# The deformable loop on clamped ramps times differences of z, with one clamp pass out of PSUM, all products of a step in one block, and a pipelined offsets stage

## What is computed

```
# off: 9 offsets (taps) for each pixel, from a depthwise conv, batch norm, relu and a 1x1 conv
def dsc_axis(x, offset, weight, axis):        # axis 'x' moves along w, 'y' along h
    ix = wb + off   (or iy = hb + off)        # position to read on the pixel's own line
    s = grid_sample_zeros(x, ix, iy)          # linear between the two neighbours, zero outside
    return einsum('bchwk,ock->bohw', s, weight)
```

## Time and profile before

| | us |
|---|---|
| median of 3 runs | 5520.23 (5514.65 to 5533.72) |
| the profiled execution: first to last instruction | 5466.7 |
| TensorE busy | 4359.0 (80%) |
| VectorE, ScalarE, GpSimd busy | 2938.9, 2478.8, 2313.4 |
| granted TensorE clock, mean | 0.854 of 2.4 GHz |
| deformable, first to last product | 1992.2 to 4979.1 |
| offsets, first load to the last store landed | 1675 to 1938 |

### The profile page before, as it was taken

One profiled execution on the slowest core, in us unless ns is written; L12 is line 12 of the kernel. 1 busy time (PEld: TensorE's weight loads), 2 busy tenths in 40 slices (PEclk: granted clock), 3 DMA queues, 4 the chain that ended last, 5 costly groups with the idle time before them and its releaser, 6 DMA issues. The chain is left out here.

```text
span 5466.7 us, 153704 instructions
## 1 busy us (share of the span) xinstructions
PE 4359.0 (80%) x59170; PEld 2491.1 (46%) x59170; DVE 2938.9 (54%) x5592; ACT 2478.8 (45%) x2871; POOL 2313.4 (42%) x1844
## 2 busy tenths in 40 slices
PE   7765584379995549999999999999999899994188
PEld 6664453323332225555555555555555555552032
DVE  5206464423333437666766766676677667665411
ACT  5401143312223426656656666566566656663111
POOL 0002100100002347767767767677677667673000
PEclk9856696589997769989889989899799999897599
DMA  3456599987774640322023203203212231015877
GB/s 94 84 107 193 126 260 265 292 204 214 214 220 166 188 74 6 61 46 53 18 42 59 52 3 61 50 2 65 46 31 38 44 57 37 18 41 154 251 172 168
DMA packets 757030, 583.81 MB, mean 107 GB/s; under 512 B 36272, under 2 KB 695216, under 8 KB 746576
## 3 DMA queue, kind: packets, MB, share of 16 engines
q1 hardware_dynamic: 604424, 419.51, 33.3%
q10 hardware_dynamic: 141984, 121.83, 7.3%
q0 software_dynamic: 9984, 33.56, 1.9%
HBM read 371.84 MB, written 202.93 MB: 105 GB/s over the span
## 5 line engine op out<-in xcount | busy, mean ns | idle before, releaser
L1412 POOL TENSOR_SCALAR df_t<-df_t 128x1536 f32<-128x1536 f32 (+1 forms) x1536 | 2042.6, 1341 | 915.0 <-ACT df_t L1452 657.0
L1452 ACT ACTIVATE df_t<-df_a 128x1024 f32<-128x1024 f32 x1536 | 1574.6, 1025 | 1136.7 <-PE df_a L1604 1113.0
L1644 PE MATMUL df_o<-df_t,df_zs 128*32 128x128 f32 x36864 | 1432.8, 291 | 64.1 <-issue 57.8
L1488 DVE TENSOR_SCALAR df_t<-df_d 128x512 int32<-128x512 int32 x1536 | 1061.0, 691 | 672.5 <-PE df_d L1604 644.8
L1644 PEld LDWEIGHTS df_o<-df_t,df_zs 128*32 128x32 f32 x36864 | 985.8, 115 | 747.7 <-issue 581.0
L1627 PE MATMUL df_z<-net_Z,df_x 32*128 32x288 f32 x4096 | 876.2, 465 | 8.1 <-DVE df_zs L1500 4.6
L1604 PE MATMUL df_a<-df_ix,net_sel 17*128 17x512 bf16 x3072 | 632.1, 406 | 27.2 <-issue 26.3
L1604 PE MATMUL df_d<-df_ix,net_sel 17*128 17x512 bf16 x1536 | 613.6, 399 | 34.6 <-DVE df_t L1488 33.5
L1627 PEld LDWEIGHTS df_z<-net_Z,df_x 32*128 32x128 f32 x4096 | 419.8, 197 | 144.9 <-DVE df_zs L1500 84.7
L1500 DVE COPY df_zs<-df_z 128x576 f32<-128x576 f32 x512 | 382.6, 747 | 4.4 <-PE df_z L1627 4.4
L1458 ACT ACTIVATE df_zs<-df_z 128x576 f32<-128x576 f32 x512 | 331.0, 646 | 62.1 <-PE df_z L1627 60.0
(11 more groups left out here) (211 smaller groups left out, 4262.2 us busy)
## 6 DMA issues: line engine op xcount, KB each, us to landing
r_x<-x SPq DMA_DIRECT2D x64, 512.0 KB, 14.3
x<-r_x ACTq DMA_DIRECT2D x64, 512.0 KB, 11.2
gc_x<-x SPq DMA_DIRECT2D x240, 128.0 KB, 4.4
dc_x<-x SPq DMA_DIRECT2D x240, 128.0 KB, 3.2
dc_xt<-x_2t SPq DMA_DIRECT2D x240, 128.0 KB, 4.7
lc_x<-x SPq DMA_DIRECT2D x112, 256.0 KB, 5.2
fw_x<-in_x SPq DMA_DIRECT2D x32, 512.0 KB, 6.6
iv_x<-in_x SPq DMA_DIRECT2D x64, 256.0 KB, 4.8
```

The costliest lines, as they stand in the source:

```text
L1412: g.tensor_scalar(t, t, 1.0, 0.0, ALU.min, ALU.max).then_inc(hat_p, 1)
L1452: act.activation(t, ps_a[(m + i) % 2][:], ACT.Abs).then_inc(a_read, 1)
L1488: v.tensor_scalar(T[:, m % 2, 3 * i + 2].bitcast(I32), ps_d[:].bitcast(I32), 0x7fffffff, None, ALU.bitwise_and).then_inc(d_read, 1)
L1644: mm = pe.matmul(ps_o[32 * q:32 * q + 32, 0:P], Zs[:, m % 2, q, 32 * k:32 * k + 32], T[:, m % 2, 3 * i + x, P * q:P * q + P], start=(k == ...
```

## The change

**The algebra.** max(0, 1 - |d|) summed over grid points against z is the same as z at the first point times one ramp plus clamped ramps min(max(d, 0), 1) times the differences of neighbouring z. So the lines are made into differences `X[:, j+1] - X[:, j]` before `make_z`, the ramp needs a relu and a cap (or one clamp), and the absolute value, the line sums, `WS` and `S` go. The first point needs 4 more products a step: `apply_first` with `Z0` (9 rows x 32 columns for each line) and `E`, the offsets clamped to 0..1 in fp32, which `offsets` now stores as `edge`. Its four products have tile positions (32q, 32q). The grid row is in the constant, so the contraction has 16 rows instead of 17.

**The steps.** VectorE clamps 4 taps as two passes of 128x1024 and one tap as a pass of 128x512, straight from PSUM; ScalarE does the other 4 taps with a relu in two passes of 128x1024 and GpSimd caps them in two of 128x1024; ScalarE copies all of z out. `ps_a`, `ps_d` and `ps_z` have one buffer each. A quarter of the steps with a = 0 turn four lines at once (`turn`, `keep`), the others none. GpSimd prepares the lines of the next half (steps 10 to 19) instead of VectorE. All loops over images are unrolled.

**The queue.** Offsets and `E` come in quarters of a half, 24 steps ahead of use (runs of 2 KB and 4 KB). The lines of the next half are loaded at the start of a half, ahead of the trip of `uy`. `move_first` sends z of the first points through DRAM at step 21.

**offsets** is unrolled and pipelined over 4 PSUM banks: ScalarE writes the bf16 part from PSUM, the bias is a third matmul with 2 rows (`gl`, `gr`), VectorE clamps `HE`, and subtracts out of PSUM, two chunks deep; the next image is loaded when TensorE has read the one before.

TensorE in `deformable`, before: one step (df_o are the products, df_a and df_d the distances of a later step, df_z the z of the next; the rows between are register work).

The core of the diff, first `offsets` (ScalarE, TensorE, VectorE):

```diff
-                        for e in range(2):
-                            for m, co in enumerate((cox, coy)):
-                                h = HI[:, k, m, N // 2 * e:N // 2 * (e + 1)]
-                                a.activation(h, h, ACT.Relu, bias=co[:, 1:2], scale=co[:, 0:1]).then_inc(relu, 1)
-                        for c in range(NCH):
-                            n = b * NCH + c
-                            a.wait_ge(full, n + 1)
-                            a.wait_ge(low, n + 1)
-                            a.activation(t_o[:, c % 2], ps_f[c % 4][:], ACT.Identity, bias=wt["pb"][:, 0:1]).then_inc(taken, 1)
...
+                    a.activation(parts[:, k, 0, r], ps_f[n % NB][:], ACT.Copy).then_inc(high, 1)
+                    if b + 1 < B and c in (3, 6):
+                        rectify(b + 1, c // 6)
...
+                    for m in range(2):
+                        pe.matmul(ps_f[n % NB][:], wt["PW"][:, m, :], HI[:, b % 2, m, 512 * c:512 * c + 512],
+                                  start=(m == 0), stop=False)
+                    pe.matmul(ps_f[n % NB][:], wt["gl"][:], wt["gr"][:], start=False, stop=True).then_inc(full, 1)
...
+                        v.tensor_scalar(HE[:, k, r], ps_f[n % NB][:], 0.0, 1.0, ALU.max, ALU.min).then_inc(edged, 1)
+                        if n >= NB:
+                            v.wait_ge(low, n - NB + 1)
+                        v.tensor_tensor(t_r[:, n % NB], ps_f[n % NB][:], parts[:, k, 0, r], ALU.subtract).then_inc(rest, 1)
```

Then `deformable`, the readers of PSUM on ScalarE and VectorE:

```diff
-                    act.activation(t, ps_a[(m + i) % 2][:], ACT.Abs).then_inc(a_read, 1)
...
+                    act.activation(t, ps_a[:], ACT.Relu).then_inc(a_read, 1)
...
-                    v.tensor_scalar(T[:, m % 2, 3 * i + 2].bitcast(I32), ps_d[:].bitcast(I32), 0x7fffffff, None,
-                                    ALU.bitwise_and).then_inc(d_read, 1)
...
+                    t = T[:, n % 2, 4 * i + 2:4 * i + 4].rearrange("p k n -> p (k n)")
+                    v.tensor_scalar(t, ps_d[:], 0.0, 1.0, ALU.max, ALU.min).then_inc(d_read, 1)
```

And its TensorE:

```diff
+                    if 2 * n + i:
+                        pe.wait_ge(a_read, 2 * n + i)
+                    for x, tap in enumerate(SCALAR[i]):
+                        mm = spread(n, tap, ps_a[:, 512 * x:512 * x + 512])
+                    mm.then_inc(a_full, 1)
...
+                    for q in range(4):
+                        pe.matmul(ps_o[32 * q:32 * q + 32, 0:P], Z0[32 * q:32 * q + K9, hh % 2, C * j:C * j + C],
+                                  E[32 * q:32 * q + K9, P * j:P * j + P], start=False, stop=False, tile_position=(32 * q, 32 * q))
...
+                    if n + 1 < ST:
+                        fill_single(n + 1)
+                        fill_scalar(n + 1, 1)
+                        fill_vector(n + 1, 1)
+                        make_z(n + 1, 1)
+                    if n >= 0:
+                        if turn_due(n) or first_due(n):
+                            pe.wait_ge(s_read, n + 2)
+                        if turn_due(n):
+                            turn(n)
...
+                        apply(n, VECTOR[0] + SCALAR[0], True, False).then_inc(half, 1)
+                        apply_first(n)
+                        apply(n, (SINGLE,) + VECTOR[1] + SCALAR[1], False, True).then_inc(applied, 1)
+                    if n + 2 < ST:
+                        fill_scalar(n + 2, 0)
+                        fill_vector(n + 2, 0)
+                        make_z(n + 2, 0)
```

More of the change, by code:

```diff
@@ new lines, in deformable @@
+        ones, prep = s.sem("ones"), s.sem("prep")
+        a_full, a_read, clipped = s.sem("a_full"), s.sem("a_read"), s.sem("clipped")
+        d_full, d_read, s_full, s_read = s.sem("d_full"), s.sem("d_read"), s.sem("s_full"), s.sem("s_read")
+        z_full, z_read, half, applied, o_read = (s.sem(n) for n in ("z_full", "z_read", "half", "applied", "o_read"))
+        turned, kept, first, first_read = (s.sem(n) for n in ("turned", "kept", "first", "first_read"))
+        z0_out, z0_in = s.sem("z0_out"), [s.sem(f"z0_in{k}") for k in range(2)]
@@ L1337, in deformable, with turns, first_due @@
+        def turns(n):
+            return sum(turn_due(m) for m in range(n + 1))
+        def first_due(n):
+            return 0 <= n and place(n)[3] == 21 and place(n)[2] + 1 < NH
         with s.block() as block:
@@ L1594, in _, with keep @@
-                with v.Fori(0, B - 1) as b:
-                    image(b, True)
-                with v.Fori(B - 1, B) as b:
-                    image(b, False)
+                        v.tensor_tensor(U[:, j], ps_o[:, 0:P], U[:, j], ALU.add).then_inc(o_read, 1)
+                def keep(n):
+                    v.wait_ge(turned, turns(n))
+                    b, a, hh, j = place(n)
+                    g = (j // 4 - 1) % 8
+                    if g == 0 and b:
+                        v.wait_ge(uy_out, 64 * b)
+                    v.tensor_copy(YB[:].rearrange("h (o l) -> h o l", o=C)[:, :, 16 * g:16 * g + 16],
+                                  ps_s[:].rearrange("h (l o) -> h o l", o=C)).then_inc(kept, 1)
@@ L1599, in _ @@
+                for c in (6, 7):
+                    stats(B - 1, c)
             @block.tensor
             def _(pe):
[L1601 to L1613 removed]
@@ L1690, in _, with spread @@
-                with pe.Fori(B - 1, B) as b:
-                    image(b, False)
+                def spread(n, tap, out):
+                    b, a, hh, j = place(n)
+                    if j % QL == 0:
+                        pe.wait_ge(q_in[j // QL], 96 * (hh + 1))
+                    e, k = divmod(tap, SLOTS)
+                    g = 32 * (2 * (j // 16) + e)
+                    return pe.matmul(out, wt["sel"][g:g + K, k, :], ixv[g:g + K, :, P * (j % 16):P * (j % 16) + P], start=True, stop=True)
@@ new lines, in make_first, with turn @@
+                def make_first(hh):
+                    pe.wait_ge(prep, 11 * hh + 2)
+                    for q in range(4):
+                        r = slice(32 * q, 32 * q + 32)
+                        mm = pe.matmul(ps_s[r, 0:N9], X0[r, hh % 2, :], WZ[r, hh % 2, :], start=True, stop=True, tile_position=(32 * q, 32 * q))
+                    mm.then_inc(first, 1)
+                def turn(n):
+                    pe.wait_ge(o_read, n)
+                    for i in range(4):
+                        mm = pe.transpose(ps_s[:, P * i:P * i + P], XO[:, (n - 4 + i) % 8], wt["eye"][:])
+                    mm.then_inc(turned, 1)
@@ new lines, in apply, with apply_first @@
+                def apply(n, taps, start, stop):
+                    for i, k in enumerate(taps):
+                        for q in range(4):
+                            mm = pe.matmul(ps_o[32 * q:32 * q + 32, 0:P], Zs[:, n % 2, q, 32 * k:32 * k + 32],
+                                           T[:, n % 2, slot(k), P * q:P * q + P],
+                                           start=(start and i == 0), stop=(stop and i == len(taps) - 1))
+                    return mm
+                def apply_first(n):
+                    b, a, hh, j = place(n)
+                    if j == 0:
+                        pe.wait_ge(z0_in[hh % 2], 64 * (hh // 2 + 1))
+                    for q in range(4):
+                        pe.matmul(ps_o[32 * q:32 * q + 32, 0:P], Z0[32 * q:32 * q + K9, hh % 2, C * j:C * j + C],
+                                  E[32 * q:32 * q + K9, P * j:P * j + P], start=False, stop=False, tile_position=(32 * q, 32 * q))
```

724 lines of the change are left out of this document (306 added, 418 removed).

## The result

The changed kernel takes 5644.1 us (median of 4 runs, 5621.9 to 5655.6) against 5517.4 us for the kernel before in the same comparison (5509.4 to 5533.7). The ratio is 1.0226, with a 95% interval of 1.0190 to 1.0261: it is 2.3% slower. The forecast was 5362 us and "faster"; its range ended at 5585. The profiled execution has a span of 5642.0 us.

What follows compares the result with a forecast made beforehand. TensorE, busy 80% of the span, was taken as the bound. Steps +76, stops and low clock -202, offsets -18, start -12, weights -2 sum to -158: 5520.2 becomes 5362 us; own range 5290 to 5450, eight in ten 5220 to 5585.

Steps and rivals of the forecast that it cites:

- the undisturbed step: TensorE's deformable step without stops: 2.7 us to the products plus a 2.57 us block, 5.27 us; +76 us in eight images.
- The second fill for ScalarE: In a deformable step, TensorE's second distances for ScalarE start at 1.50 us, after waiting 0.3 us for its pass.
- VectorE's pair pass: VectorE's pass over 1024 columns of distances in a deformable step: taken as 1.2 us, between 1.02 and 1.38.
- Extra work of turns, `keep`, statistics and first points: Occasional delays in the deformable stage, added to the 64 steps of each image: 8 + 3.2 + 2 us.
- the long stops: TensorE's 6 us standstills inside distances, laid to code held back by 16 KB packets; 2 KB runs should leave none.
- the term of -202 us: Deformable stage: standstills and the low clock behind them shrink from 272 to 70 us; bounds 14 and 272 left.
- a clock near 0.98: Sign that the forecast holds: the deformable stage's clock near 0.98, with no stop of 6 us.
- The clock falls: Rival: TensorE's waits amid distances and z bring 1.2 GHz in a fifth of steps; +445 us, 5807 us; 6%.
- Offsets: Pipelined offsets stage: 27 us an image, 263 to 245 us in all, -18 us; bounds -42 and +22.
- Start: Gap of 54.2 us between offsets and first product: -12 us, bounds -25 and +10; first points' trip may delay it.
- The trip of `uy`: Now queued behind the next half's lines, so GpSimd may get it late: 0 to 7 us, taken as 2.
- the pair of waits behind the readers: Readers' second passes were to hide under products; a rival had one more wait of 0.3 us a step, +150 us, 7%.

Runs made afterwards that it cites:

- two-block run with one wait: Changed kernel with each step's products in two blocks, the second waiting until ScalarE has read the distances just filled: 5287.3 us, ratio 0.955 to the kernel before.

## Why the prediction was wrong

**Right, nearly to the hundredth: the undisturbed step.** Forecast 2.7 us from the first distances to the products, measured 2.73; block 2.57, measured 2.59; step 5.27, measured 5.33. The second fill for ScalarE starts 1.50 us into the count, as forecast, the one for VectorE 1.92 (1.88). VectorE's pair pass, which no row showed and which was taken as 1.2 us between bounds of 1.02 and 1.38, is 1.22. Extra work of turns, `keep`, statistics and first points: forecast 13.2 us an image, 106 in eight; measured 104 (the stretches' sum above 512 x 2.73).

**Right: the long stops go.** No stop over 2.3 us is left in the stage, and of 12 steps longer than 11 us one is left. Two causes went at once, the long packets and the loop's jump back; the prediction had priced the first. The row that it read for it, 101 packets in the earlier trace rows, is of 3128 to 3134, the 6 us ahead of the stop and not the stop itself; from 3134 to 3140 the same queue fills 85% of the 16 engines.

**Wrong: the term of -202 us.** It let the low clock go with the stops, down to 70 us of stops and low clock, "a clock near 0.98". Measured: a clock of 0.87, and 350 us more than undisturbed over the blocks, 329 of them at the low clock. The stage was forecast at about 2860 us and took 3180: this is the whole of the miss (+320 of the 333 us between 5309 and the span of 5642). The step that failed is the one from "the low clock of before stands behind stops" to "without stops it is gone". That was read from the kernel before, where TensorE hardly waits in a step, and even there it left out the three places without a stop. The same prediction had put 0.5 us of waits into every step, in one row with the lightest work, and had costed them as time only.

**The rival "The clock falls" was the case, given 6%.** It had the place right and was dismissed by a row that did not fit: the axis y stretch of the earlier trace rows with a wait in each step. There the step was cut by three blocks of products, and the two-block run with one wait shows that even a longer wait can leave the clock alone in such a step. Its size was off in both directions: not a fifth but two fifths of the steps, and not 4.35 us each but 1.55, because the low clock mostly lies over the block alone and is gone in the 2.73 us behind it.

**Small terms.** Offsets: forecast 245 us, measured 263.5, the same as before. The DMA share rose from 0.59 to 0.65 only, so the pipeline ran no closer to the transfers; within the bounds given (-42, +22). Start: 54.2 became 32.4 (-21.8, forecast -12), and 11.3 us of it came back as the wait for the first points in the first step, as feared there. The trip of `uy` and the pair of waits behind the readers stayed hidden.

The loss against before is then: undisturbed steps 512 x 5.33 + 104 = 2833 against 2716 (+117), and 350 us over the blocks against 272 of stops and low clock (+78). Together that is +195, where the stage measures +192. The start gives back 22 and small terms take 5, so the span is 175 us longer.

**Where the expected gain went.** The other parts of the change are good: with the products split in two, they are worth some 570 us. The one block spent it all, 0.66 us of waits and some 0.2 us of lost overlap in each step, and some 330 us of clock.

## What to carry to other kernels

A bound engine that is given a wait in each step doesn't only lose the wait: on TensorE, price its heavy work at both rates of the clock, and check whether waits and the lightest work have been put into one stretch. Split the heavy work so that each of its parts covers the readers of what was filled just before; two parts were enough here, and a third only cost. A cheap test of a clock theory is to fill the waits with matmuls that nobody reads: if the time falls, it was the clock.

## What the runs showed of the hardware that I had not expected

- More work, less time: 2048 records more on TensorE (65538 against 63490) took 270 us off, at an unchanged 5.33 us per undisturbed step; the stage's clock went from 0.87 to 0.97.
- Less work, more time: 0.14 us less in each step cost 164 us, with the clock at 0.81.
- Waits of 0.6 to 1.0 us in every step left the clock at 0.96 when the products stood in two blocks; in the kernel before, with three blocks, the clock fell at three places behind waits of 0.3 us.
- Distances and z on different groups of rows run side by side: 0.69 us for a fill that takes 0.93 on the same groups.
- With packets of 2 KB in place of 16 KB the stops of 6 us inside the distances went, but the six stops of some 4 us at the loop's jump back stayed, and the time did not move.
